# One sum of eight key tiles per group, its last two addends by accumulating transfers from GpSimd's queue

## The reference, cut to what matters

```
q = (x @ Wq + bq)                      # 2 x 512 x 512, 16 heads of 32
k = (y @ Wk + bk);  v = (y @ Wv + bv)  # y: 2 x 8192 x 384
scores = einsum('bnhd,bmhd->bhnm', q, k) / sqrt(32)
attn = softmax(scores, axis=-1)
out = einsum('bhnm,bmhd->bnhd', attn, v)
```

## Time and profile before

| what | us |
|---|---|
| median of three runs | 3074.13 (3073.68 to 3076.14) |
| the profiled execution, its own time | 3071.63 |
| its span, first to last instruction | 3069.8 |
| TensorE busy | 2977.9 |
| GpSimd busy | 1962.5 |
| attention: GpSimd's first and last work of a group | about 110 to 2268 |

### The profile page before, as it was taken

The page is one execution under the profiler, slowest core; times in us unless marked ns, Lnnn a source line. Parts: engine busy times, 40 slices in busy tenths (PEclk is TensorE's granted clock), DMA queues, the critical chain, the costliest instruction groups (busy, mean ns, idle before and its releaser), DMA issues.

```text
span 3069.8 us, 40867 instructions
## 1 busy us (share of the span) xinstructions
PE 2977.9 (97%) x15216; PEld 1818.9 (59%) x15216; DVE 2220.0 (72%) x3368; ACT 1679.1 (55%) x2920; POOL 1962.5 (64%) x682
## 2 busy tenths in 40 slices
PE   7999999999999999999999999999999877899999
PEld 4666666666666666666666666666534333344477
DVE  7777777777777777777777777777746899986653
ACT  1566666666666666666666666666641555320021
POOL 1699898989989898988989898989850000000000
PEclk9999999999999999999999999999999989999999
DMA  6423332232223233332223222332240122224100
GB/s 165 122 53 78 71 76 63 63 85 67 73 53 90 61 94 98 76 86 53 73 61 91 56 70 66 85 74 53 47 156 29 43 68 97 67 70 166 69 14 18
DMA packets 99817, 230.10 MB, mean 75 GB/s; under 512 B 22754, under 2 KB 27874, under 8 KB 98114
## 3 DMA queue, kind: packets, MB, share of 16 engines
q1 hardware_dynamic: 99044, 226.71, 27.8%
q10 hardware_dynamic: 576, 0.79, 0.1%
HBM read 114.46 MB, written 8.06 MB: 40 GB/s over the span
## 4 chain that ended last, share of the span: by engine, by line
PE 90%; DVE 6%; ACT 1%; POOL 1%; issue 1%; DMA 0%; SPq 0%; ACTq 0%; DVEq 0%; POOLq 0%
PE ps L1819 17%; PE ps L1858 15%; PE ps L1845 15%; PE ps L1772 9%; PE ps L1796 9%; PE ps L1803 9%; PE ps L2065 4%; PE ps L2029 4%; PE ps L1873 4%; PE ps L2045 3%; DVE bx L1308 1%; PE ps L1827 1%; POOL psum L896 1%; PE ps L2057 1%; ACT V L1516 1%
## 5 line engine op out<-in xcount | busy, mean ns | idle before, releaser
L1046 DVE TENSOR_REDUCE pm<-ps 128x1 f32<-128x512 f32 x2048 | 1407.4, 691 | 571.7 <-PE ps L1819 499.1
L1527 ACT ACTIVATE pf<-ps 128x512 f32<-128x512 f32 x2048 | 1216.6, 599 | 721.8 <-PE ps L1845 626.7
L896 POOL TENSOR_TENSOR psum<-psum,pf 128x2048 f32<-128x2048 f32 x254 | 1167.7, 4597 | 70.3 <-ACT pf L1527 57.7
L1819 PE MATMUL ps<-ks,qs 96*128 96x512 f32 x2048 | 844.0, 412 | 4.9 <-DVE pm L1046 2.3
L1845 PE MATMUL ps<-qs,ks 98*128 98x512 f32 x2048 | 812.8, 398 | 2.8 <-ACT pf L1527 2.6
L896 POOL TENSOR_TENSOR psum<-pf 128x2048 f32<-128x2048 f32 x127 | 581.5, 4579 | 80.2 <-ACT pf L1527 79.0
L1819 PEld LDWEIGHTS ps<-ks,qs 96*128 96x128 f32 x2048 | 386.6, 189 | 262.6 <-issue 198.7
L1858 PE MATMUL ps<-pf,V 128*32 128x512 f32 x4096 | 492.7, 598 | 0.0
L1845 PEld LDWEIGHTS ps<-qs,ks 98*128 98x128 f32 x2048 | 390.6, 191 | 50.0 <-ACT pf L1527 12.4
L908 POOL PARTITION_ALL_REDUCE qstat<-qstat x2 | 0.7, 366 | 608.5 <-DVE qstat L1344 608.5
L1796 PE MATMUL ps<-cTh,Wkg 128*128 128x512 f32 x732 | 292.7, 400 | 2.6
(11 more groups left out here) (223 smaller groups left out, 3004.3 us busy)
## 6 DMA issues: line engine op xcount, KB each, us to landing
ks<-KH SPq DMA_DIRECT2D x512, 128.0 KB, 2.4
ks<-KL SPq DMA_DIRECT2D x256, 128.0 KB, 2.4
cT<-in_ctxT SPq DMA_DIRECT2D x32, 768.0 KB, 4.8
Wkg<-wk_rows SPq DMA_DIRECT2D x61, 384.0 KB, 3.1
BC<-bc_rows SPq DMA_DIRECT2D x32, 512.0 KB, 4.8
ring<-in_ffn_w SPq DMA_DIRECT2D x16, 1024.0 KB, 7.8
wA<-in_W_fcT SPq DMA_DIRECT2D x4, 1024.0 KB, 10.0
wB<-in_W_projT SPq DMA_DIRECT2D x4, 1024.0 KB, 7.0
```

Source lines behind the costliest of these rows:

```text
L896: pool.tensor_tensor(acc, before, pf[:, tile % P_SLOTS, :], ALU.add).then_inc(s_sum, 1)
L1046: dve.tensor_reduce(pm[:, n // BLK, n % BLK:n % BLK + 1], src, AX.X, ALU.max).then_inc(s_wfree, 1)
L1527: act.activation(pf[:, tile % P_SLOTS, j * NTOK:(j + 1) * NTOK], ps[:, S_BANK + u % S_BANKS, :], ACT.Exp, scale=SCALE).then_inc(s_exp, 1)
L1819: last = pe.matmul(dst, qs[0:3 * HD, h, t * P:(t + 1) * P], ks[0:3 * HD, keys_of(of, j), i * 512:(i + 1) * 512], start=True, stop=True)
```

## The change

- One sum takes a whole group's eight tiles. GpSimd makes five additions (tiles 0 to 5; `ADDS`), and tiles 6 and 7 are added to `psum` by two transfers that GpSimd's own queue issues (`pool.dma_start` with `accum_op=ALU.add`, 128 by 2048 numbers from `pf` onto `psum`). The second waits until the first has landed, since both read and write the same bytes. `rescale` stands between the two.
- `sums(g)` runs once in a group, not twice. It waits for both transfers and stands behind the burst two bursts (half a group) after the group's last one (`SUM_BURST`).
- `pf` has five slots. The exponentials that reuse a slot of tile 6 or 7 wait for the transfer that read it.
- `low_context` stands ahead of the first and the fifth addition of the second group of a chunk, `keep_max` behind the third addition.
- The denominators' turn "D" comes 16 steps later (`D_LAG` 17), and `save_out(0)` stands behind `max_rows` on SyncE.
- The last group adds three tiles only and keeps `last_sums` for the other four, as before.

```diff
-D_LAG = 1
+D_LAG = 17
-LOW_AT = {2: (0, 0), 3: (1, 2)}
-P_SLOTS = 4
+LOW_GROUP = 1
+LOW_AT = {0: 0, 4: 1}
+P_SLOTS = 5
-NSUM = 4
+TAIL = 2
+ADDS = MT - 1 - TAIL
+KEEP_ADD = 3
+LAST_SUMMED = 4
+SUM_BURST = MT // BURST + TAIL
...
+            for g in range(NGT):
+                adds = ADDS if g < NGT - 1 else LAST_ADDS
+                acc = psum[:, g % 2, :]
+                if g >= 2:
+                    pool.wait_ge(s_den, g - 1)
+                for n in range(adds):
+                    if low_at(g, n):
+                        low_context(*low_at(g, n))
+                    tile = g * MT + n + 1
                     pool.wait_ge(s_exp, HG * (tile + 1))
                     before = pf[:, (tile - 1) % P_SLOTS, :] if n == 0 else acc
                     pool.tensor_tensor(acc, before, pf[:, tile % P_SLOTS, :], ALU.add).then_inc(s_sum, 1)
...
+                if g < NGT - 1:
+                    for n in range(TAIL):
+                        tile = g * MT + ADDS + 1 + n
+                        pool.wait_ge(s_exp, HG * (tile + 1))
+                        if n > 0:
+                            pool.wait_ge(s_tail, 16 * (g * TAIL + n))
+                        pool.dma_start(acc, pf[:, tile % P_SLOTS, :], accum_op=ALU.add).then_inc(s_tail, 16)
+                        if n == 0:
+                            rescale(g)
...
+                    if r <= ADDS:
+                        act.wait_ge(s_sum, of * ADDS + max(r, 1))
+                    else:
+                        act.wait_ge(s_tail, 16 * (of * TAIL + r - ADDS))
...
-            def sums(run):
+            def sums(g):
...
+                if g < NGT - 1:
+                    pe.wait_ge(s_tail, 16 * (g + 1) * TAIL)
+                else:
+                    pe.wait_ge(s_sum, g * ADDS + LAST_ADDS)
```

More of the change, by code:

```diff
@@ L166, in high_at, with low_at @@
     return [(c, half, f) for f in range(KC)] if half is not None and c < NB * NCH else []
[L169 to L173, removed]
+def low_at(g, n):
+    c = g // NG + 1
+    if g % NG == LOW_GROUP and n in LOW_AT and c < NB * NCH:
+        return c, LOW_AT[n]
+    return None
 LEAD_SIDE, LEAD_WORK, LEAD_IN = lead_in()
@@ L727, in _ @@
                     max_rows(g + 1)
+                if g == NGB:
+                    save_out(0)
                 if g == NGT - 2:
@@ L1861, in values @@
                 last.then_inc(s_pv, 1)
-            def sums(run):
-                g, r = divmod(run, MT // NSUM)
-                first = run % CHUNK_RUNS == 0
-                if run == 0:
+            def sums(g):
+                first = g % NG == 0
+                if g == 0:
                     pe.wait_ge(s_sel, NG + 1)
-                if first and run > 0:
-                    pe.wait_ge(s_dt, run // CHUNK_RUNS)
-                pe.wait_ge(s_sum, (run + 1) * ADDS)
+                if first and g > 0:
+                    pe.wait_ge(s_dt, g // NG)
+                if g < NGT - 1:
+                    pe.wait_ge(s_tail, 16 * (g + 1) * TAIL)
+                else:
+                    pe.wait_ge(s_sum, g * ADDS + LAST_ADDS)
                 for j in range(HG):
                     last = pe.matmul(ps[j * HD:(j + 1) * HD, DEN_BANK, :], sel[:, g % NG, :],
-                                     psum[:, run % 2, j * NTOK:(j + 1) * NTOK], start=first,
-                                     stop=(run % CHUNK_RUNS == CHUNK_RUNS - 1))
+                                     psum[:, g % 2, j * NTOK:(j + 1) * NTOK], start=first,
+                                     stop=(g % NG == NG - 1 and g < NGT - 1))
                 last.then_inc(s_den, 1)
             def last_sums():
-                for tile in range(NGT * MT - NSUM, NGT * MT):
+                for tile in range(NGT * MT - MT + LAST_SUMMED, NGT * MT):
                     for j in range(HG):
@@ L1891, in burst @@
                         values(tile)
-                run, rest = divmod(BURST * n, NSUM)
-                if n > 0 and rest == 0 and run < RUNS:
-                    sums(run - 1)
+                g, rest = divmod(n - SUM_BURST, MT // BURST)
+                if g >= 0 and rest == 0:
+                    sums(g)
                 if n == BURSTS - 1:
+                    sums(NGT - 1)
                     last_sums()
```

36 lines of the change are left out of this document (10 added, 26 removed).

## The result

The changed kernel took 3190.52 us (median of four runs, 3189.51 to 3193.64), the kernel before on the same chip 3075.14 (3073.68 to 3076.24): a ratio of 1.0377, with a 95% interval from 1.0359 to 1.0395. The forecast was 3023, its range 3014 to 3150. The time lies 167 us above the forecast and outside the range.

The account below looks back on a forecast made before the run. TensorE was taken as the bound, busy for 97% of the span, with GpSimd next. 3071.6 - 54.2 (products removed) + 2.5 (end) + 1 (saved accumulator) = 3020.9 us; the median lies 2.5 above: 3023, range 3014 to 3150.

Parts of the forecast that it names:

- What leaves TensorE: Attention on TensorE: 63 denominators' runs of 0.86 us vanish without a wait, 54.2 us gained; turn 34.30 to 33.44 us.
- T and c: First accumulating transfer, issue to landing, T = 6.7 us; second issue holding GpSimd, c = 1.0; sum 7.7, hidden under 7.8.
- old time: GpSimd's turn: at T + c = 8.7 us it reaches the earlier 34.30 us; beyond, each us costs 1 us a turn.
- wrong as a whole: Accumulating transfers: the prediction fails entirely if a 1 MB one takes over 8 us.
- The rest of GpSimd's turn: GpSimd's turn without T + c: five additions 23.2, maxima 0.6, context 1.75, together 25.6 us.
- The heavy turn: Turn with the context's 7.0 us: GpSimd some 5 us late; following turns take 33.3 less 1.75 us and recover it.
- The slots: Reuse of the probabilities' slots: transfers land at 41.3 and 48.0 us of a turn, in time with T up to about 7.
- tile 12: Exponential reusing tile 7's slot: could start at 50.2 us, in time by 2.2; 2.8 late in the turn with 7.0 us context.
- Other transfers late: Rival on key stacking: the traffic delays other transfers and TensorE waits for keys; 1 us a turn, 3085 us; chance 0.03.
- The end: End of the attention: the chain through GpSimd grows from 28.1 to 31.0 us, costing 2 to 3 us once.
- GpSimd becomes the bound: Rival on GpSimd's turn: T = 8.3, c = 1.5, turn 35.4 us, 3146 us; chance 0.30, of which 0.15 beyond 3150.
- its signs: Turns over 34.3 us, no GpSimd idle time ahead of additions or maxima, exponentials or denominators waiting for transfer or GpSimd.

Follow-up runs that it names:

- plain-transfer run: Changed kernel with its 126 accumulating transfers as plain copies onto the sum, so the denominators are wrong: 3031.73 us (one execution).
- no transfer: Sum of eight tiles a group by seven GpSimd additions, one denominators' product a group, five slots, against the changed kernel's two transfers: 3191.61 us (one execution).
- one adding: Changed kernel with one accumulating transfer a group instead of two, six additions by GpSimd, five slots: 3047.93 us, ratio 0.9925.
- heavy turn made even: Changed kernel, two of five additions in the turn with both context pieces cut to a quarter of their columns (denominators wrong): 3094.21 us, ratio 1.0067.
- the same, six slots: Changed kernel with those two additions cut to a quarter of their columns, plus six slots for the probabilities instead of five: 3086.37 us, ratio 1.0043.
- short stacking: Changed kernel whose key-stacking transfers carry an eighth of their columns from the seventh group on (scores wrong): 3142.17 us (one execution).

## Why the prediction was wrong, step by step

**What leaves TensorE: right.** The burst without denominators is followed by the next product at once. The chain from 900 to 1000 us, one burst of each kind (answers to the earlier trace rows):

```profile
912.88 1.85 PE ps L1872 x16
914.73 0.86 PE ps L1889 x8
915.59 0.43 PE ps L1833
...
921.69 1.85 PE ps L1872 x16
923.55 0.43 PE ps L1833
```

The plain-transfer run, 39 us under the kernel before on its chip, bears the sum out: turns of 33.59 where 33.4 was forecast, though transfers and the waits around them are still in it.

**T and c: the single transfer right, the interval not.** The forecast had 6.7 us to the landing, by doubling the data part. The quickest landed after 7.0, the plain one after 4.3 (median 4.7). The earlier trace rows gave 4.0 for a plain one, so the doubling holds. The Trainium skill's rule ("Collectives: The Full Stack", Part 3, the bandwidth ceiling: told there of a reduce-scatter, which reads two sources and runs at half the rate of the copying all-gather) agrees with these rows. But the first landings averaged 7.56 (up to 11.8), and the second issue started 8.1 us behind the first on average: the landing and 0.55 us more, which the forecast had at nothing. The scaling's waits for VectorE (44.2 us in 12 places, at "D") lie within the landing, hidden as the forecast had said: with "D" six steps earlier the interval stayed 8.1. c was 0.6, not 1.0. T + c was thus 8.7 and not 7.7. By the forecast's own threshold that alone would have eaten the gain: 8.7 was its "old time". The median landing of both transfers, 8.0, stands at the 8 us beyond which the forecast called itself wrong as a whole.

**The rest of GpSimd's turn: too small.** The forecast had 25.6 - 1.75 = 23.85 us. The rows show, from the start of the first addition to the first issue, 4.97 + 9.3 + 0.6 + 9.3 + 0.3 = 24.5, as the addition beside a transfer's start takes 4.9 and not 4.6 us, and a pause of 0.3 stands ahead of each issue. An ordinary turn by these rows: 8.1 + 0.6 + 24.5 = 33.2. The wait for the maxima (1.36 us in the earlier trace rows) is not in this sum. The forecast took it for idle time that GpSimd can give up, and that was right: with six slots it shrank to 0.08 us in the two intervals in which GpSimd is behind.

**The heavy turn: the step that failed.** "The following turns take 33.3 less 1.75 us and win it back." That is 31.55, 1.9 under TensorE's 33.44. What they take can be measured: from 400 to 2230 us, take off each interval between two maxima rows what GpSimd waited for others (for maxima and tiles, and ahead of the second issue all that goes beyond the landing and 0.55 us). At the four places of a chunk 32.9, 36.2, 35.8 and 32.9 us are left, 34.4 in the mean. The two in the middle have one half of the context work each. They put GpSimd 5.1 us behind TensorE, just as the forecast said ("some 5 us"), but an ordinary interval wins back 0.6 us and not 1.9. So by these rows some 34.4 us a turn is the least that GpSimd allows, 1.0 over the forecast or 62 us in all, and it is late in every chunk. The measured turn is 36.05. The further 1.6 us come from what this lateness and the traffic set off: exponentials that wait for the slot, the first product for the maxima that waits for keys, and the slower clock behind both. No run splits them cleanly, since each edit moves the others. The edits that take a term out of GpSimd's chain give back nearly all: no doubling, 33.59; no heavy turn, 34.47.

**The slots: the reasoning right, the landing not.** The forecast gave tile 12 a reserve of 2.2 us with landings of 6.7. The second took 9.1 on average, and 10.7 behind a heavy turn, in the stacking of keys. That the forecast saw that overlap and dismissed it ("for which GpSimd doesn't wait") is an error of its own: the exponentials do wait. It cost 19 us by the run with six slots.

**Other transfers late: the rival at 0.03 had a part.** It was priced at 1 us a turn, 3085, and put aside since "keys are stacked two groups ahead". The scores read them later, but the first product for a group's maxima reads them at once: 3.7 us behind the landing in the rows above, before, and 2.1 at the least from 400 to 2230 us. With two adding transfers in a turn the stacking takes some 13 us from its first issue to its last landing instead of 9.7, and the margin is mostly gone. On the page of the changed kernel, against 2.4 in the earlier trace rows:

```profile
ks<-KH SPq DMA_DIRECT2D x512, 128.0 KB, 3.6
```

Counted in the traces from 400 to 2230 us (us):

| run | stacking, first issue to last landing | TensorE's waits | of these, ahead of the first product for maxima |
|---|---|---|---|
| before | 9.7 | 0.3 | 0 |
| no transfer | 9.8 | 86.7 | 0 |
| two plain ones | 10.3 | 10.2 | 0.2 |
| one adding | 11.0 | 17.1 | 9.1 |
| changed kernel | 13.7 | 84.3 | 19.4 |
| six slots | 12.9 | 71.0 | 54.2 |
| heavy turn made even | 13.0 | 36.8 | 24.7 |
| the same, six slots | 12.8 | 35.0 | 35.0 |

That the waits are for keys follows from the 0.09 us between landing and product, and from their absence with the short stacking (0 of TensorE's 62.2 us there). How many us the keys cost in the changed kernel isn't measured alone: the short stacking gave back 44 us and also shortened the second landing.

**The end: mis-sized.** 9.0 us more instead of 2.5. The last two accumulating transfers stand in the chain with 11.79 and 6.99 us:

```profile
2360.08 11.79 DMA psum<-pf
...
2372.40 6.99 DMA psum<-pf
```

**The rival "GpSimd becomes the bound" was the greater part of what happened**, but it was priced by T + c = 9.8 alone and without the unevenness, at 3146. Most of its signs were there: turns over 34.3 us, exponentials waiting for the transfer. One sign did not hold as written: GpSimd keeps idle time ahead of the maxima (4.25 us in the rows above), when TensorE has been held up and brings the maxima late. That this idle time is a consequence is argued from the order of events; no run took it away alone.

**Left open.** How the 1.6 us a turn above GpSimd's own 34.4 divide among slot, keys and clock. A run that starts the stacking of keys earlier, beside an even turn and six slots, would show whether the forecast's 33.4 can be reached with adding transfers. It was not tried.

## What to carry to other kernels

Add up the program of an in-order engine from row to row, pauses included, and not by the busy time of its instructions. Where one turn in four is heavy, compare the longest turn and what the next ones can truly win back, not the mean. When a bound is lifted and the time hardly moves, look at what the busiest engine now waits for: here it was keys, delayed by the new traffic, and no longer the engine that the theory named. For each transfer that runs beside the new ones, look for its earliest reader; keys stacked two groups ahead had one 2 to 4 us behind their landing. A transfer that another instruction of the same queue has to wait for costs its whole landing; one such transfer, for which GpSimd does not wait, was worth 0.8 to 0.9% here, two in a row cost 4%.

## What the runs showed of the hardware

- An accumulating 1 MB transfer from GpSimd's queue within SBUF lands after 7.0 us at best and 8.0 in the median, a plain one after 4.3 and 4.7. It holds GpSimd 0.87 us (the plain one 0.57 to 0.59) in its own row, but the next instruction starts 0.60 behind its start. That next one is slower: an addition 4.9 us instead of 4.58, a scaling 1.4 instead of 1.08.
- Beside these transfers SyncE's queue gets slower too: a 128 KB transfer that stacks keys landed after 3.6 us in the median instead of 2.4, and SyncE's issue of one took 0.89 us in the mean and 2.85 at most, instead of 0.60 and 2.28. With plain transfers the landing stayed 2.4.
- A VectorE instruction on 128 by 16 numbers can take 4.4 us instead of 0.17. With seven additions on GpSimd it averaged 2.0 us (count, busy, mean ns):

```profile
L1086 DVE TENSOR_SCALAR nm<-mn 128x16 f32<-128x16 f32 x53 | 108.1, 2040 | 1.8
```

  The Trainium skill has the rule ("SBUF — State Buffer", SBUF: two separate sides: the pair of ports that VectorE and GpSimd share is an exclusive lock for a whole instruction). The trace agrees: the row above of 2.10 us ends at 1013.96, when the addition that ran beside it ends (1013.92), and the same values by a TENSOR_REDUCE took 0.17 us. The prediction had cited that page for the other direction only, VectorE holding up GpSimd.
- Behind a stop of TensorE of 3.6 us stood 5 us at a granted clock of 0.52, in the rows above. Over 600 us, 26 us of waits in all went with 44 us lost, 14 of them by the granted clock.
